# Adapter weights picked by 64 one-hot products, or copied item by item from a turned table

## The reference

```python
hidden = gelu(einsum('bsd,ad->bsa', x, down_W) + down_b)
expert_out = einsum('bsa,boa->bso', hidden, Wsel) + bsel[:, None, :]
domain_output = where(valid[:, None, None], expert_out, hidden)
hidden = domain_output + domain_emb[idx][:, None, :]
x = layernorm(einsum('bsa,da->bsd', hidden, up_W) + up_b + x)
```

## Time and profile before

| | us |
|---|---|
| median of 3 runs | 622.02 |
| lowest, highest | 619.15, 623.5 |
| span of the profiled execution | 614.2 |
| TensorE busy in the span | 541.9 (88%) |
| VectorE, ScalarE, GpSimd busy | 379.6, 278.0, 242.0 |

### The profile page before, as it was taken

The page is one execution under the profiler, slowest core; times in us unless marked ns, Lnnn a source line. Parts: engine busy times, 40 slices in busy tenths (PEclk is TensorE's granted clock), DMA queues, the critical chain, the costliest instruction groups (busy, mean ns, idle before and its releaser), DMA issues.

```text
span 614.2 us, 15656 instructions
## 1 busy us (share of the span) xinstructions
PE 541.9 (88%) x4402; PEld 457.1 (74%) x4403; DVE 379.6 (62%) x1233; ACT 278.0 (45%) x628; POOL 242.0 (39%) x208
## 2 busy tenths in 40 slices
PE   5987969778646997979999999999999999999993
PEld 3764756576443886858888888888888888898782
DVE  2566978978886775518775454555556464644542
ACT  3548755756652743322345253434343343434431
POOL 2001387778777047262234242323323232424322
PEclk8679787868957998999999999999999999999998
DMA  9455436564533524434354444452524242323212
GB/s 250 147 174 172 171 115 219 160 211 130 191 122 113 121 38 95 39 95 53 53 103 79 76 78 60 41 65 35 69 35 68 35 59 44 49 37 54 38 26 27
DMA packets 78091, 57.54 MB, mean 94 GB/s; under 512 B 51346, under 2 KB 71699, under 8 KB 77907
## 3 DMA queue, kind: packets, MB, share of 16 engines
q1 hardware_dynamic: 63698, 38.37, 24.4%
q0 software_dynamic: 13296, 17.83, 17.1%
q10 hardware_dynamic: 1058, 0.85, 0.8%
HBM read 23.18 MB, written 24.55 MB: 78 GB/s over the span
## 4 chain that ended last, share of the span: by engine, by line
PE 68%; DVE 10%; POOL 7%; issue 6%; ACT 4%; DMA 3%; another core or an unknown queue 1%; SPq 1%; ACTq 0%; DVEq 0%; POOLq 0%
PE banks L808 30%; PE banks L824 29%; DVE stats L1133 3%; POOL queues L561 3%; PE banks L640 2%; PE banks L713 2%; POOL rs L552 2%; ACT hT L910 1%; POOL rsT L569 1%; DVE w_low L1216 1%; DMA out<-hT,token 1%; PE banks L721 1%; DMA uw<-up_b 1%; PE banks L700 1%
## 5 line engine op out<-in xcount | busy, mean ns | idle before, releaser
L592 POOL DMA_INDIRECT out<-hT,token x71 | 114.7, 1615 | 242.7 <-ACT hT L1014 203.3
L808 PE MATMUL banks<-nb,w_high 128*128 128x256 f16 (+1 forms) x1248 | 195.6, 263 | 2.8 <-issue 1.7
L824 PE MATMUL banks<-w_high,stage 128*128 x1136 | 190.4, 274 | 1.6 <-issue 0.9
L808 PE MATMUL banks<-nb,w_low 128*128 128x256 f16 (+1 forms) x624 | 162.6, 263 | 0.4 <-issue 0.4
L824 PE MATMUL banks<-w_low,stage 128*128 x568 | 155.6, 274 | 1.1 <-issue 1.1
L998 ACT ACTIVATE xb<-banks,feat 128x256 f32<-128x256 f32 (+1 forms) x312 | 120.0, 454 | 56.9 <-PE banks L808 31.6
L808 PEld LDWEIGHTS banks<-nb,w_high 128*128 x1248 | 114.2, 98 | 21.7 <-issue 5.2
L824 PEld LDWEIGHTS banks<-w_high,stage 128*128 128x128 f16 x1136 | 110.9, 98 | 16.4 <-issue 3.1
L1014 ACT ACTIVATE hT<-act,gate 128x256 f32<-128x256 f32 x71 | 32.6, 501 | 183.0 <-DVE act L1478 183.0
L1451 DVE CAST stage<-xb 128x512 f16<-128x512 f32 (+1 forms) x156 | 66.5, 426 | 60.5 <-ACT xb L998 31.7
L1453 DVE TENSOR_TENSOR stage<-xb,stage 128x512 f16<-128x512 f32 (+1 forms) x156 | 100.6, 645 | 5.4
(11 more groups left out here) (186 smaller groups left out, 547.5 us busy)
## 6 DMA issues: line engine op xcount, KB each, us to landing
stage<-expert_w SPq DMA_DIRECT2D x32, 512.0 KB
xb<-x SPq DMA_DIRECT2D x8, 512.0 KB
out<-rb SPq DMA_DIRECT2D x8, 512.0 KB, 3.3
queues<-pad_row SPq DMA_DIRECT2D x9, 260.0 KB
out<-hT,token POOLq DMA_INDIRECT x71
queues<-h_rows,slot POOLq DMA_INDIRECT x64
rb<-exp_b SPq DMA_DIRECT2D x1, 1024.0 KB, 4.8
nb<-queues SPq DMA_TRANSPOSE x39
```

Of the source, the lines that this page charges most:

```text
L592: nc.gpsimd.indirect_dma_start(out=out, out_offset=bass.IndirectOffsetOnAxis(ap=token[:, i.par, s:s + 1], axis=0), in_=yg[:, i.par, s, :], ...
L808: last = nc.tensor.matmul(ps_in(i, c), w[:, at], features(i)[:, v, k, :], start=(n == 0), stop=(n == 3 * DC - 1))
L824: last = nc.tensor.matmul(ps_out(i.par)[:, s, :], v[:, i.par, c, s * P:(s + 1) * P], w[:, at], start=(n == 0), stop=(n == 3 * FC - 1))
```

## The change

The table is loaded in another layout, with the output index in the 64 partitions, and 16 products with an identity matrix turn the adapters into two banks (`turn_table`). VectorE and ScalarE copy one bank each to `turned`, GpSimd adds the identity for items without an adapter. `wsel` is now a small buffer for two groups. For each group, SP reads each of its eight items' numbers into a register and issues a transfer of 64 partitions x 256 B from `turned` to `wsel` (`load_adapters`). Those of group 0 come ahead of round 0, those of group g+1 at the head of round g's SP work, ahead of its weight loads. The down product of group 0 comes ahead of the turning, the products for the item rows behind it. The rounds cut 6, 4, 4 and then 3 chunks. The gelu table is loaded ahead of the first work of ScalarE.

```diff
-CUTS = [8, 3, 3, 3, 3, 3, 3, 3, 3]
+CUTS = [6, 4, 4, 3, 3, 3, 3, 3, 3]
...
+                def load_adapters(i):
+                    wait(sp, adapt_done, i.g - 1)
+                    for b in range(GI):
+                        item = i.g * GI + b
+                        no = sp.value_load(adapter_no[0:1, item:item + 1], min_val=0, max_val=NONE_ROW)
+                        sp.dma_start(wsel[:, i.par, b, :], turned[:, bass.ds(no * A, A)]).then_inc(adapters_loaded[i.par], 16)
+
                 load_x(At(0, 0))
+                for dst, src in ((dw[:], down_w), (ab[:, 0:1], down_b)):
+                    sp.dma_start(dst, src).then_inc(down_loaded, 16)
...
                 load_weights(At(0, 0), slice(2, STAGES))
+                sp.wait_ge(adapters_known, 1)
+                sp.wait_ge(turned_copied, N_TURNED)
+                load_adapters(At(0, 0))
 
                 def body(i):
+                    if i.g + 1 < GROUPS:
+                        load_adapters(At((i.g + 1) // 2, (i.g + 1) % 2))
                     if i.g == 1:
                         sp.wait_ge(cleared_zero, 1)
...
-                def select():
...
+                def turn_table():
+                    pe.wait_ge(table_loaded, 16)
+                    for n in range(ADAPTERS):
+                        last = nc.tensor.matmul(banks[0:A, 4 + n // 8, (n % 8) * A:(n % 8 + 1) * A], table[:, n, :],
+                                                ident[0:A, 0:A], start=True, stop=True)
+                        if n % 8 == 7:
+                            last.then_inc(table_turned, 1)
...
+                    if i.g > 0:
+                        add_item_rows()
+                    else:
+                        pe.wait_ge(down_loaded, 16 * N_DOWN)
...
                     if i.g == 0:
-                        select()
-                        for w in range(2):
-                            pe.wait_ge(select_copied[w], SELECTS)
+                        turn_table()
+                        item_rows()
+                        pe.wait_ge(dom_row, 2)
+                        pe.wait_ge(net_ready, 2)
+                        add_item_rows()
...
+                    pe.wait_ge(adapters_loaded[i.par], (i.half + 1) * GI * 16)
                     pe.wait_ge(act_ready, i.g + 1)
...
                     if i.g == 0:
-                        cut_high(i, slice(0, 1))
                         activate(s1)
-                        for b in range(SELECTS):
-                            cut_high(i, slice(b + 1, b + 2))
-                            copy_selected(b)
+                        copy_turned()
+                        cut_high(i, slice(0, 2))
                         adapted(s1)
-                        cut_high(i, slice(SELECTS + 1, None))
+                        cut_high(i, slice(2, None))
                         return
```

More of the change, by code:

```diff
@@ L61 @@
 assert EARLY * SLOTS <= 2 * FIRST * GROUP - EXPERTS * (SLOTS - 1) and EARLY % 2 == 0
+TABLE, TURNED = CHUNKS - 5, CHUNKS - 3
+assert CUTS[-1] == CHUNKS - TURNED and (NONE_ROW + 1) * A * 2 <= (CHUNKS - TURNED) * CHUNK
 W2_AT = EXPERTS * DC * FF
@@ L219, in program @@
         token = sb("token", [P, 2, SUB], U32)
+        wsel = sb("wsel", [A, 2, GI, A])
+        adapter_no = sb("adapter_no", [1, ITEMS], I32)
         gate = sb("gate", [P, 2, SUB])
@@ L223, in program @@
         share = sb("share", [P, SUB])
-        table = w_low[0:NONE_ROW + 1, 16 * CHUNK:24 * CHUNK].bitcast(F32)
-        wsel = w_low[0:A, 24 * CHUNK:32 * CHUNK].bitcast(F32)
-        wsel_pairs = wsel.rearrange("a (i q w) -> a w q i", q=A // 2, w=2)
+        table = w_low[0:A, TABLE * CHUNK:(TABLE + 2) * CHUNK].bitcast(F32).rearrange("o (e a) -> o e a", a=A)
+        turned = w_low[0:A, TURNED * CHUNK:CHUNKS * CHUNK].bitcast(F32)
         scratch = w_high[:, 24 * CHUNK:32 * CHUNK].bitcast(F32)
@@ L667, in adapter, with add_item_rows @@
                 def adapter(i):
[L668 to L676, removed]
+                    def add_item_rows():
+                        wait_apart(pe, dom_row, (dom_ready, i.g))
+                        wait(pe, place_ready, i.g - 2)
+                        nc.tensor.matmul(ps_dom, item_add[:], bcast(ident[:, bass.ds(i.g * GI, GI)], 2, [P, GI, T]),
+                                         start=True, stop=False)
+                    if i.g > 0:
+                        add_item_rows()
+                    else:
+                        pe.wait_ge(down_loaded, 16 * N_DOWN)
                     wait(pe, logits_copied, i.g - 2)
@@ L682, in adapter @@
                     if i.g == 0:
-                        select()
-                        for w in range(2):
-                            pe.wait_ge(select_copied[w], SELECTS)
+                        turn_table()
[3 more added lines that the diff above has]
+                        add_item_rows()
                     if i.g == 1:
                         style_layer(3)
+                    pe.wait_ge(adapters_loaded[i.par], (i.half + 1) * GI * 16)
                     pe.wait_ge(act_ready, i.g + 1)
                     for b in range(GI):
-                        item = i.g * GI + b
-                        last = nc.tensor.matmul(ps_dom[:, b * T:(b + 1) * T], wsel[:, item * A:(item + 1) * A],
+                        last = nc.tensor.matmul(ps_dom[:, b * T:(b + 1) * T], wsel[:, i.par, b, :],
                                                 act[:, b * T:(b + 1) * T], start=False, stop=(b == GI - 1))
@@ L896, in activate @@
                     wait(sc, adapt_done, i.g)
-                    if isinstance(i.g, int) and i.g == 0:
-                        sc.wait_ge(early_loaded, 16 * N_EARLY)
+                    if i.g == 0:
+                        sc.wait_ge(down_loaded, 16 * N_DOWN)
                     nc.scalar.activation(act[:], ps_down, ACT.Gelu, bias=ab[:, 0:1]).then_inc(act_ready, 1)
@@ L982, in body @@
                         scale_features(s2)
[L984 to L986 removed]
+                sc.dma_start(table, adapter_w[0:ADAPTERS].rearrange("e (o a) -> o e a", a=A)).then_inc(table_loaded, 16)
+                nc.scalar.preload_act_table(ACT.Gelu)
                 for dst, src in ((hw1, hyp_w1), (feat[:], feature), (hw2, hyp_w2), (sw1, sty_w1), (sw2, sty_w2),
@@ L1353, in body @@
                     if i.g == 0:
-                        cut_low(i, slice(0, 1))
-                        for b in range(SELECTS):
-                            copy_selected(b)
-                            cut_low(i, slice(b + 1, b + 2))
+                        cut_low(i, slice(0, 2))
                         row_constants()
-                        cut_low(i, slice(SELECTS + 1, None))
+                        cut_low(i, slice(2, None))
                         return
```

50 lines of the change are left out of this document (19 added, 31 removed).

## The result

| | before | after |
|---|---|---|
| median, both on one chip, 7 runs each | 621.08 us | 625.25 us |
| lowest, highest | 617.18, 623.72 | 622.42, 630.8 |
| span of the profiled execution | 614.2 us | 620.6 us |

The ratio is 1.0104, with a 95% interval of 1.0069 to 1.0138: 6.5 us (4.3 to 8.6) slower. The two spans differ by 6.4, the two medians by 4.2, just under that interval. By each of them the changed kernel is slower, by 0.7 to 1%. Of the runs further down, one execution of h_more_loads_late took 805 us at a granted clock of 0.63 and is left out of every number of that run.

The account below looks back on a forecast made before the run. The experts were taken as bound by TensorE, the first 199 us as a chain of waits. Round 1's 7.0 us late plus round 2's 1.2 gave 8.2: span 622.4, plus 7.8 to the median, 630.2 us, range 619 to 637.

Parts of the forecast that it names:

- Down product first: Start of the kernel: ScalarE has the features at 8.90 us and group 0's down product ends at 10.4.
- Turning: Turning the adapter table: sixteen products take 2.3 to 3.9 us, a bank's copy 1.03; SP can begin at 14.2.
- The pair: SP's register load and transfer for one item: 1.22 us, likely bounds 1.10 and 1.37, unlikely 0.68.
- Round 0: Group 0's adapters landed at 26.6 us, its up product over at 35.7, 4.1 us earlier than before.
- Into round 1: ScalarE after round 0's last cuts: chunks 4 and 5 wait for SP, features copied at 39.7 us, where 40.81 was.
- Chunk 6: Round 1's first chunk: issued at 45.2 us, landing at 48.5; gelu at 49.6 (45.18 before), up product ending 56.2 to 60.1.
- The other arm: Round 1's cuts and `layer_norm`, starting at 55.0 us; turning of group 0's rows taken at 58.6, 7.0 us late.
- The fourth cut of round 2: One more low cut on VectorE ahead of round 2's routing: 1.16 us, entered as 1.2.
- Rounds 3 to 6: Weight loads behind eight more pairs, first chunk landing 13.9 us after the store: nothing in the sum, up to 1 us in the range.
- SP isn't the bound: Rival: SP's register load and transfer cost as little as 0.68 us, and the kernel is faster, 616 us; chance 0.12.
- The two cancel: Rival: 0.80 to 1.10 us per load and transfer, or faster chunk landing; sums -2 to +5, likeliest 623.7 us; chance 0.23.
- SP is late in each round: Rival: 1.5 us per load and transfer, 1 to 2 us more in each of rounds 3 to 6; 641 us; chance 0.10.

Follow-up runs that it names:

- h_more_loads_late: The changed kernel with a second, unused register load for each item of groups 4 to 7: 633.02 us, ratio 1.023 to the kernel before.
- b: The changed kernel without the register loads, each transfer taking its adapter from a constant address: 596.02 us, ratio 0.9863 to the kernel before.
- e: The kernel before, selection kept, with the down product of group 0 and its loads first: 614.42 us, ratio 0.9902.
- l: e with the changed kernel's cuts of 6, 4, 4: 602.99 us, ratio 0.9982 to the kernel before.
- c: The changed kernel with the cuts as before the change (8, 3, 3): 610.35 us, ratio 1.01 to the kernel before.
- f: The changed kernel with groups 0 to 2's adapters copied by GpSimd, SP's weight loads ahead of later groups' pairs: 609.6 us, ratio 0.981.
- i: a with 15 added float16 products in round 1's wait for the gelu and 5 ahead of its up product: 618.64 us, ratio 0.9995.
- n: k with SP's pairs ahead of the round's weight loads from round 2 on: 602.55 us, ratio 0.9761 to the kernel before.
- a: The changed kernel with weight loads (from round 2 only the first) ahead of the next group's pairs in SP's queue: 603.43 us, ratio 0.9964.
- k: f with group 3's adapters copied by GpSimd too: 593.3 us, ratio 0.9812 to the kernel before.
- d_warm_round_1: The changed kernel with 24 and 12 added float16 products in round 1, behind the turning of x and ahead of the adapter products: 610.89 us, ratio 1.0115.

## Why the prediction was right, step by step

The direction, the place and the size held: 630.0 was predicted, in 619 to 637, and 625.25 came. Against its own before the change cost 6.5 us by the ratio, for the 8.2 of the sum. Of the 5.0 us between 630.2 and 625.25 only 1.8 are the span's (622.4 for 620.6). The other 3.1 are the step from the span to the median, taken over from the kernel before at 7.8 and here 4.7.

1. *Down product first.* It ended at 8.8, for 10.4. The wait for its bias was 0.41. The 1.6 us are the features': they were ready at 7.17 (6.09 + 1.08), for 8.90, because TensorE turned x at 5.46 and not at 7.15. In all eleven kernels with the turned table that is at 5.1 to 5.6, in the three with the selection at 6.9 to 7.5, where TensorE waits for x. The prediction had kept the place of x from the kernel before; what brings x sooner wasn't tried.
2. *Turning.* 2.08 us, a little under the lower bound of 2.3, and the copy of a bank 0.59, for 1.03. SP's first register load started at 11.6, not 14.2: of the 2.6, 1.6 are step 1's.
3. *The pair.* The 1.22 taken from two rows held, and not the 0.68 of their durations. A steady pair is 1.18; with the slow ones among them, the 24 took 29.1 us of the queue (11.6 to 41.80 less 1.1 for chunks 4 and 5), 1.21 each. b shows that the sum hangs on it: at 0.66 the kernel came to 8.3 us under its before, where the rival had worked out 6.
4. *Round 0.* Adapter products at 22.56, for 26.6; the up product over at 30.9, for 35.7. The start, 2.6 of it, was step 2. 16 KB land in some 1.3 us (the last issue of group 0 ends at 21.3), for 2.6. The gain over before is 9 us, not 4.1. This is the term that was furthest off, and it didn't reach the time, because chunk 6 came after it.
5. *Into round 1.* Chunks 4 and 5 at 31.3, for 33.7; features at 37.2 to 38.3, for 39.7. "3 of the 4 us are gone": 5.4 of 9 were (37.22 is 3.6 ahead of 40.81).
6. *Chunk 6.* Issued at 42.97, for 45.2; it landed by 47.66, so in 4.7 us, for 3.3. The earlier issue and the slower landing nearly cancel: gelu at 48.62, for 49.6. Then the up product ran at half clock throughout, the far end of the range that was given (7.1 us).
7. *The other arm.* `layer_norm` started at 53.62, for 55.0. The turning came at 59.95, for 58.6: 8.4 late for 7.0. That this is nearly the sum is luck in part, for everything up to the gelu was 1 us early and the clock took it back.
8. *The fourth cut of round 2.* 1.13 us by e and l, for 1.16; the lag grew by 1.7. The mechanism is right only where SP leaves room: in c the cut was gone, and a wait of 2.17 stood there.
9. *Rounds 3 to 6.* They took 21.0, 20.0, 20.0 and 20.1 us, before 21.0, 20.2, 20.7 and 20.1: hidden, as said. h puts the room at 1.5 to 1.9 us where step 9's comparison was 1.1 short.

What the sum lacked is the end. The lag shrank from 10.1 to 8.8 in rounds 3 to 8 and to 6.4 in the tiles of experts. TensorE is full from 286 us on the earlier trace rows, but it isn't in the first tiles, and "whatever moves the end of the front moves the end of the kernel by as much" was too strong for this chip. It shows in f too, which took 420.0 us from its front to its end where e, on the same chip, took 416.8, and h, with the latest front there, 413.4. In the traces of before, after, e, f, h, i and n TensorE stands, 42 to 48 us behind the front, for 2.5 to 6.7 us at the turning behind the last router products, and goes on at half clock (1.94 us for 1.07). The other seven have no such wait, and they took 402.2 to 403.6 whatever the front: there c and b lie 16.0 us apart at the front and 16.3 at the end, as the prediction has it. TensorE in the changed kernel, in f and in l:

```profile
250.51 1.94 PE L744 MATMUL banks<-ident,xT 128*128 128x128 f32 x8 [3.28 <-ACT lg L940]
```

```profile
239.20 1.94 PE L763 MATMUL banks<-ident,xT 128*128 128x128 f32 x8 [6.71 <-ACT lg L959]
```

```profile
237.25 1.07 PE L730 MATMUL banks<-ident,xT 128*128 128x128 f32 x8 [0.38 <-ACT lg L926]
```

What makes that wait on some chips isn't known. So that 6.4 lies near the 8.2 of the sum is luck in part: 10.1 stood at round 3, and 3.7 were given back where the sum had nothing.

Of the rivals, "SP isn't the bound" was that of a cheap pair, and b is that kernel. "The two cancel" would have needed 0.95 us a pair. "SP is late in each round" failed on its price, 1.18 for 1.5; but h shows that its point of decision lay only some 0.2 us a pair above what the pair costs, since 1.5 to 1.9 us are shared by eight.

On the register load: the Trainium skill, "DMA: Bandwidth & Descriptors", section "Latency and other measured facts", gives a floor of some 600 ns. Of the 64 rows of the changed kernel 55 have 262 to 299 ns for the load alone and nine 402 to 866, and h has 0.55 us for the load with its check and address steps. The measured row decides for the load; for the queue the price is nearer to the page's than to the row's.

## What to carry to other kernels

Before moving work from an engine to a transfer, price what the issuing queue pays for each, from the end of one issue to the end of the next and not by the durations of its rows, and list what stands behind it in that queue. A gain that ends before the next wait of that queue is not a gain. Try the order of the queue and an idle engine too: against the changed kernel the order alone was worth 7.7 us of the front (a), and copies on GpSimd 19.8 (k). When limits stand in a row, removing one shows only what lies before the next. a mended the queue in round 1 and met the clock; i mended the clock as well and met the queue in round 2. Look where the next round begins, not only at the place that was mended.

## What the runs showed of the hardware

- A register load on SP with what belongs to it takes 0.55 us of the queue, though its row says 0.27; with the issue of a transfer behind it, 1.18 us, 1.21 on average of 24. GpSimd's load and a copy of 64x64 float32 take 0.68 us, of which the copy is 0.23.
- A transfer of 64 x 256 B from `turned` to `wsel` landed some 1.3 us after the end of its issue. From the start of the issue to the landing the median was 1.7 us in d_warm_round_1, and 2.3 in b_no_register, where the issues follow each other at 0.66. A chunk of 512 KB with 1.5 MB behind it took 4.7, for the 3.3 of a store alone.
- In the changed kernel TensorE stood idle for 8.38 us up to 40.63 and was at half clock behind it (the product with `item_add` 1.97 us, for 1.07 in a_weights_first). With one more wait of 2.83 us it stayed there: 0.52 was granted from 49.4 to 60.0, through 10 us of float32 products. In a_weights_first a wait of 3.27 us was enough, with the products ahead of it at the full clock and the adapter products behind it at half (1.79 us). With 15 float16 products of 128x512 in place of that wait and 5 ahead of the up product (i_clock_kept) the clock stayed at 1.00. With 24 and 12 in other places (d_warm_round_1) it held for the adapter products alone.
- The kernel before took 605 us on some chips and 620 on others. Fronts can be compared across them, to a few us; times can't.
